# Moving two transposes behind half of a product, and a down projection in 17 matmuls

## What is computed

```python
Q, K, V = xpos(X @ W_Q), xpos(X @ W_K, downscale=True), X @ W_V
p = softmax(Q @ K.T) * 0.9 ** abs(n - m)          # 1024 x 1024 for each sequence
x = layernorm(X + p @ V)
def fp4_linear(x, w):                             # blocks of 16: scale = max(abs)/6, values on a grid of 8
    return einsum('bsk,nk->bsn', fp4(x), fp4(w))
h = silu(fp4_linear(x, w_gate)) * fp4_linear(x, w_up)    # 704 wide
out = layernorm(x + fp4_linear(h, w_down))
```

## Time and profile before

| | us |
|---|---|
| median of the runs | 1100.65 |
| lowest and highest | 1100.05, 1101.77 |
| the profiled execution | 1102.91 |
| its span, first to last instruction | 1101.1 |
| busy: PE / PEld / DVE | 1024.1 / 954.6 / 979.6 |
| busy: ACT / POOL | 469.2 / 688.1 |

### The profile page before, as it was taken

The page is one execution under the profiler, slowest core; times in us unless marked ns, Lnnn a source line. Parts: engine busy times, 40 slices in busy tenths (PEclk is TensorE's granted clock), DMA queues, the critical chain, the costliest instruction groups (busy, mean ns, idle before and its releaser), DMA issues.

```text
span 1101.1 us, 19638 instructions
## 1 busy us (share of the span) xinstructions
PE 1024.1 (93%) x6820; PEld 954.6 (87%) x6820; DVE 979.6 (89%) x2147; ACT 469.2 (43%) x883; POOL 688.1 (62%) x653
## 2 busy tenths in 40 slices
PE   5559999999999999999999999999999999999975
PEld 4458899899999989899999989999998999989964
DVE  6956999999999999999999999999999999999974
ACT  3232444444444444444434444534444444444432
POOL 3573676667666575857657676756757676565542
PEclk9769999999999999999999999999999999999987
DMA  5210011111012010211012010210111110000000
GB/s 190 75 63 25 11 58 38 50 39 58 21 37 70 20 59 11 78 40 46 23 39 78 15 54 20 78 34 16 58 39 51 37 59 20 15 17 19 21 15 19
DMA packets 28177, 47.20 MB, mean 43 GB/s; under 512 B 2864, under 2 KB 21552, under 8 KB 26032
## 3 DMA queue, kind: packets, MB, share of 16 engines
q1 hardware_dynamic: 27264, 45.17, 13.0%
q10 hardware_dynamic: 816, 0.79, 0.2%
HBM read 37.55 MB, written 8.39 MB: 42 GB/s over the span
## 4 chain that ended last, share of the span: by engine, by line
PE 75%; DVE 14%; POOL 5%; issue 2%; ACT 2%; DMA 1%; SPq 0%; POOLq 0%; DVEq 0%; ACTq 0%
PE ps_g L400 10%; PE ps_g L402 10%; PE ps_g L401 10%; PE ps_t L409 6%; PE ps_o L400 6%; PE ps_o L402 6%; PE ps_o L401 6%; PE ps_y L402 4%; PE ps_y L401 4%; PE ps_y L400 4%; DVE hsc L807 3%; PE ps_s L400 3%; PE ps_s L402 3%; PE ps_s L401 3%; POOL h L1170 2%
## 5 line engine op out<-in xcount | busy, mean ns | idle before, releaser
L1170 POOL TENSOR_TENSOR h<-h,hsc 128x704 f32<-128x704 f32 x128 | 178.2, 1392 | 244.0 <-DVE h L1026 194.7
L400 PE MATMUL ps_g<-wgu_h,xqt_h 128*128 128x352 f32 x512 | 171.3, 335 | 2.9 <-DVE h L960 2.0
L402 PE MATMUL ps_g<-wgu_h,xqt_l 128*128 128x352 f32 x512 | 165.6, 323 | 0.0
L401 PE MATMUL ps_g<-wgu_l,xqt_h 128*128 128x352 f32 x512 | 165.4, 323 | 0.0
L1262 POOL TENSOR_TENSOR prob<-prob,decay_t 128x512 f32<-128x512 f32 x128 | 162.3, 1289 | 2.9 <-ACT prob L707 2.9
L400 PE MATMUL ps_o<-v_h,pt_h 128*128 128x256 f32 x512 | 151.8, 296 | 5.3 <-DVE pt_l L830 5.3
L402 PE MATMUL ps_o<-v_h,pt_l 128*128 128x256 f32 x512 | 146.6, 286 | 0.0
L401 PE MATMUL ps_o<-v_l,pt_h 128*128 128x256 f32 x512 | 146.4, 286 | 0.0
L671 ACT ACTIVATE th<-ps_g 128x352 f32<-128x352 f32 x128 | 59.5, 465 | 171.8 <-PE ps_g L402 171.8
L400 PE MATMUL ps_s<-k_h,q_h 128*128 128x512 f32 x256 | 107.2, 419 | 9.9 <-DVE k_l L938 9.9
L400 PE MATMUL ps_y<-wd_h,ht_h 128*128 128x256 f32 x384 | 109.7, 286 | 1.4 <-DVE ht_l L837 1.4
(11 more groups left out here) (186 smaller groups left out, 2916.0 us busy)
## 6 DMA issues: line engine op xcount, KB each, us to landing
rope_t<-rope SPq DMA_DIRECT2D x16, 1024.0 KB, 5.3
xin<-x_t SPq DMA_DIRECT2D x16, 512.0 KB, 4.0
xres<-x SPq DMA_DIRECT2D x64, 128.0 KB, 2.0
out<-yout SPq DMA_DIRECT2D x64, 128.0 KB, 1.9
decay_t<-decay SPq DMA_DIRECT2D x1, 960.0 KB, 4.8
h<-w_down SPq DMA_DIRECT2D x2, 352.0 KB, 4.6
prob<-w_k ACTq DMA_DIRECT2D x1, 256.0 KB, 3.2
prob<-w_q ACTq DMA_DIRECT2D x1, 256.0 KB, 6.4
```

Source lines behind the costliest of these rows:

```text
L400: pe.matmul(dst, a_h, b_h, start=(start and i == 0), stop=False)
L401: pe.matmul(dst, a_h, b_l, start=False, stop=False)
L402: mm = pe.matmul(dst, a_l, b_h, start=False, stop=(stop and i == n - 1))
L1170: return tt(blocks(dst), blocks(src), sc[:, which, :].unsqueeze(2).to_broadcast([P, n, QB]), ALU.mult)
```

## The change

- PE issues the two transposes of `xv` between the two halves of PV (where there is a tile `prev`), no longer ahead of them. The wait on `r2_done` goes from there.
- `xe` moves from `ps_o` to the second half of `ps_y`, the place of `ps_xqt`. ACT waits on `r2_done` ahead of it instead of on `xgrid_done`.
- The padded half of the last chunk of h and of `w_down` no longer holds zeros but a second copy of the last 64 values. In the transposed h, rows 64 to 127 of chunk 5 get the low part in place of the high part (a second subtraction on VectorE, 64 partitions, into `ht_h`), so that one matmul does high x high and low x high, and a second over 64 rows high x low: 17 matmuls instead of 18. `ht_l` has five chunks.
- POOL writes the quantised h in three instructions instead of one: the copy of the last 64, columns 0 to 511, columns 512 to 703, with `hq_done` after each of the two last and a wait of its own on `hcopy_done`. PE waits for either half ahead of the transposes that read it.
- In the set-up, the weights' rows are copied likewise, and the memset of the padding goes.

```diff
-        ht_l = sb("ht_l", [P, FC, P], F32R)
+        ht_l = sb("ht_l", [P, FC - 1, P], F32R)
...
-        xe = ps_o[:, D:2 * D]
+        xe = ps_y[:, D:2 * D]
...
-                    pe.wait_ge(pad_zero, 1)
...
+            def down():
+
+                product(ps_y[:, 0:D], [(ht_h[:, n, :], ht_l[:, n, :], wd_h[:, n, :], wd_l[:, n, :])
+                                       for n in range(FC - 1)], None, stop=False)
+                pe.matmul(ps_y[:, 0:D], ht_h[:, FC - 1, :], wd_h[:, FC - 1, :], start=False, stop=False)
+                pe.matmul(ps_y[:, 0:D], ht_h[0:LAST, FC - 1, :], wd_l[0:LAST, FC - 1, :], start=False, stop=True)\
+                    .then_inc(y_done, 1)
...
-                if gu.ok():
-
+                def x1_transposes():
                     wait(pe, xq_done, gu.n(1, 1))
-                    wait(pe, r2_done, fin.n())
                     if gu.n() == 0:
 
                         pe.wait_ge(wtl_done, WG)
                     transposes(ps_xqt, [xv[:, a * P:(a + 1) * P] for a in range(DH)], xqt_done)
+
+                if gu.ok() and not prev.ok():
+                    x1_transposes()
...
                     product(ps_o[:, 0:D], over_keys(range(NT // 2)), None, stop=False)
-
+                    if gu.ok():
+                        x1_transposes()
                     wait(pe, ptl_done, prev.n(2, 2))
                     product(ps_o[:, 0:D], over_keys(range(NT // 2, NT)), o_done, start=False)
...
-                    product(ps_y[:, 0:D], [(ht_h[:, n, :], ht_l[:, n, :], wd_h[:, n, :], wd_l[:, n, :])
-                                           for n in range(FC)], y_done)
+                    down()
                 if dn.ok():
 
-                    wait(pe, hq_done, dn.n(1, 1))
+                    wait(pe, hq_done, dn.n(2, 1))
                     if prev.ok():
                         wait(pe, ptl_done, prev.n(2, 2))
                     transposes(ps_t[:, 0], [h[:, dn.slot % 2, n * P:(n + 1) * P] for n in range(4)], ht_done)
+                    wait(pe, hq_done, dn.n(2, 2))
                     transposes(ps_t[:, 1], [h[:, dn.slot % 2, n * P:(n + 1) * P] for n in range(4, FC)], ht_done)
...
-                    wait(act, xgrid_done, gu.n())
+                    wait(act, r2_done, fin.n())
...
-                lo, n = ((0, 4), (4, 2))[g]
+                lo, n = ((0, 4), (4, 1))[g]
                 wait(dve, hth_done, tile.n(2, g + 1))
-                tt(ht_l[:, lo:lo + n, :], ps_t[:, g, 0:n], ht_h[:, lo:lo + n, :].bitcast(F32),
-                   ALU.subtract).then_inc(htl_done, 1)
+                ins = tt(ht_l[:, lo:lo + n, :], ps_t[:, g, 0:n], ht_h[:, lo:lo + n, :].bitcast(F32), ALU.subtract)
+                if g == 1:
+                    ins = tt(ht_h[LAST:P, FC - 1, :], ps_t[LAST:P, 1, 1, :], ht_h[LAST:P, FC - 1, :].bitcast(F32),
+                             ALU.subtract)
+                ins.then_inc(htl_done, 1)
...
-            nc.vector.memset(h[:, :, F:FP], 0.0).then_inc(pad_zero, 1)
...
-                        wait(dve, hq_done, dn.n())
+                        wait(dve, hq_done, dn.n(2))
...
+                if n >= FC:
+                    times_scale(h[:, n - FC, F:FP], v[:, F - LAST:F], sc, 0, F - LAST).then_inc(hcopy_done, 1)
+                    pool.wait_ge(hcopy_done, n - FC + 1)
...
-                    times_scale(hv, hv, hsc, 0).then_inc(hq_done, 1)
+                    h_row = h[:, dn.slot % 2, :]
+                    times_scale(h_row[:, F:FP], h_row[:, F - LAST:F], hsc, 0, F - LAST).then_inc(hcopy_done, 1)
+                    times_scale(h_row[:, 0:CW], h_row[:, 0:CW], hsc, 0).then_inc(hq_done, 1)
+                    wait(pool, hcopy_done, dn.n(1, 3))
+                    times_scale(h_row[:, CW:F], h_row[:, CW:F], hsc, 0, CW).then_inc(hq_done, 1)
```

## The result

The changed kernel takes 1138.25 us (median), the kernel before 1100.84; the ratio is 1.0334, 95% interval 1.0313 to 1.0354: slower by 3.3%. One of the four executions of the changed kernel took 1668.97 us at a mean granted clock of 0.569; the ratio leaves it out, the median is over all four. The profiled execution took 1137.92 us with a span of 1136.1, 35.0 us more than the span before. Forecast were 1143 and a range from 1118 to 1166.

What follows compares the result with a forecast made beforehand. Both TensorE and VectorE were taken as full, VectorE's program order deciding; step delays of 40.5 us plus early steps, start and tail made 42 us, on the median of 1100.65 us giving 1143, range 1118 to 1166.

Steps and rivals of the forecast that it cites:

- The bound: Whole kernel: TensorE and VectorE both full to within half a microsecond, VectorE working strictly in program order.
- TensorE's wait changes its name: At PV: the 22.9 us of waits for `xv` are not removed; another semaphore ends the wait at the same moment.
- signs of the list: Expected profile: VectorE waits some 45 us for `xqt_h`, TensorE waits for `pt_l` instead of `xv`, its busy share 90% or less.
- Lengths of the steps: From one `silu(dn, 1)` on VectorE to the next: plain (without projection) 15.08 us, key 17.04, value 16.86, query 16.72.
- Splitting ht_l: VectorE's subtraction becomes two instructions: 0.06 us more a step with usual overlap, 0.22 with none, taken as 0.14.
- 17 matmuls: Down projection: 0.12 us less in each of 64 tiles, 7.7 us of TensorE time, worth nothing where VectorE sets the step.
- This is the largest term: The transposes' move delays VectorE's `xqt_low` and all behind it: plain steps +1.22 us, value and query +0.62, key 0.
- the two terms of the splits: In each step's chain: 0.48 us for POOL's h in three pieces, 0.14 for the split of ht_l on VectorE.
- "0" for the key step: Key steps: VectorE itself reaches `xqt_low` only at 7.84 us, so no delay; the step stays 17.04 us.
- That TensorE sets the pace: Rival: the 22.9 us of waits and 7.7 us of matmuls go, 1070 us; chance 0.09.
- The milder case: Rival: plain steps lose as worked out, value and query steps stay: 1127 us, or 1115 to 1125; chance 0.12.
- The clock: Rival: idle TensorE drops to its lower level, at most 1.6 us per plain step: up to 1174, about 1160; chance 0.08.

Runs made afterwards that it cites:

- low_on_top: Changed kernel with the low part of the last chunk in partitions 0 to 63 instead of 64 to 127, the last matmul reading rows 64 to 127: 1125.27 us.
- splits_only: Changed kernel with the transposes put back ahead of PV, everything else of the change kept: 1128.28 us, ratio 1.0248 to the kernel before.
- move_only: Kernel before with only the transposes moved between the halves of PV, the magnitude in `ps_y` and ACT's wait on `r2_done`: 1115.27 us, ratio 1.0124.
- full_rows: splits_only with the last of the 17 matmuls over all 128 rows instead of 64: 1112.52 us, ratio 1.0109 to the kernel before.
- ordered versions: Three kernels with the move and VectorE's order fitted to it, the last also with 17 matmuls, all over 128 rows: 1084.50, 1081.04 and 1078.18 us.

## Why the prediction was right, and where not

- **The bound.** Right for the changed kernel: inside the batches VectorE has no idle time there between `xqt_low` and the end of a step. For the kernel before it was a loop of both engines, with 75% of the chain on TensorE. The decisive reading was the order in VectorE's timeline, not its 89%. A wait of 1.53 us before `xqt_low` was forecast as 1.47, its start as 5.72 and measured as 5.75.
- **TensorE's wait changes its name.** Right: PV waits for `pt_l` and starts 3.39 us into the plain step. Two signs of the list came out otherwise. VectorE's waits for `xqt_h` were 69.4 us instead of some 45: 1.5 us in plain steps, as forecast, but 1.49 in value steps instead of 0.9, and 0.89 in query steps instead of 0.7. TensorE's busy share stayed at 93% instead of 90% or less, for the reason given with the totals.
- **Lengths of the steps.** 15.08, 17.04, 16.86 and 16.72 were forecast, 14.89 (14.81 in the last batch), 16.92, 16.80 and 16.66 measured. The difference lies in the tail behind `xqt_low`: 9.36 forecast, 1069.38 - 1060.32 = 9.06 measured. Three terms were mis-sized. POOL's h starts 3.42 behind `xqt_low` instead of 3.58, since the magnitude is ready (1060.95) long before `h_shift` starts now (1061.85). The three pieces took 1.74 until `rs1`, not 1.87. From `x1` to `h_low` it was 1.12, not 1.27. Against them stands the step from `h_low` to the next, 2.20 instead of 2.09.
- **Splitting ht_l.** Taken as 0.14, the middle; it was the upper end, 0.22 and a little more (1.95 became 2.20). The rule of the Trainium skill that the prediction names held and should have had more weight than a middle of two bounds; low_on_top shows its price as 13 us in this kernel.
- **17 matmuls.** Wrong in the cost, without effect on the forecast, which is luck. I took 0.12 us saved for each tile, with the 64-row matmul at the price of a full one; it was 0.15 lost. That VectorE sets the step hid it, as the prediction said of the saving; in splits_only, where TensorE counts, it was 15.8 us with what hangs on it.
- **"This is the largest term."** Wrong as an attribution. The sum was made of delays along one chain, and I gave the whole of the chain to the move. Alone, the move costs 14 us and the splits 27. Without the two terms of the splits (0.48 and 0.14) the same chain gives 14.46 for a plain step, 16.42 for a key step, 16.24 and 16.10 for value and query; move_only has 14.47, 16.51, 16.55 and 16.37. So the chain is right in plain and key steps and too short in value and query ones, where `xqt_low` starts at 8.03 and 7.85 in move_only and not at 7.66 and 7.52. On top of the move the splits add 0.25 to 0.42 us a step, not 0.62. The forecast lies 5 us over the measured time because the two errors have opposite signs; that part is luck. It is so too with "0" for the key step: it held a gain of 0.53 from the move and a loss of 0.41 from the splits, and that VectorE alone set its length before is wrong.
- **The rivals.** That TensorE sets the pace (1070) fell. It becomes true once VectorE's list is fitted: 1081 us (TensorE busy 835.98 of 836 us). The milder case, value and query steps unchanged, fell too: they became 0.55 us longer. The clock stayed at 0.974; TensorE's waits in plain steps were 0.78 us, not 1.9, and did it no harm. The price of that rival was too high besides: it took 0.13 us a matmul from the durations, where the starts stand 0.21 apart instead of 0.12 (1056.16 and 1056.37 in the kernel before, at a granted clock of 0.50), so 12 matmuls cost 1.1 us and not 1.6.

Open: how much of the gain of the ordered versions the new order would give without the move, and why full_rows has 17.22 in key steps (TensorE waits 1.08 us a step for `xv` there, 0.75 in the kernel before; the cause behind that was not taken apart).

## What to carry to other kernels

Where two engines are both near 90%, find for the moved work the instruction that waits for it in the other engine's own queue, and write down what stands behind that: it is delayed by the whole move, whatever slack the moved work has. Move the waiting instruction along with it, kind of step by kind of step, since the same exchange made one kind 0.3 us shorter and another 0.5 longer. Cutting an instruction up costs on each engine that gets the pieces; price them in the neighbours' distances, not in durations.

## What the runs showed of the hardware

- A matmul over 64 rows in a stream of 128-row ones started 0.21 us behind its predecessor and held its follower for 0.31, against 0.12 and 0.13 over 128 rows: 0.27 us dearer than the full one, over rows 0 to 63 and over rows 64 to 127 alike.
- A VectorE instruction that starts at partition 64 between others that start at 0 lost the overlap on both sides, 0.23 us together.
- A `tensor_scalar` of 44 columns took 1.49 us instead of 0.18 while a POOL instruction of 2.4 us ran, and ended with it; placed at the end of that instruction it took 0.18.
